# A second folding of the softmax exponentials on GpSimd in a decoder layer

## The chip, the cores and the metric

The kernel runs on one core of a Trainium2 chip. The metric is the device time of one execution in microseconds (us); the time before is the median of three runs. The trace comes from one further, profiled execution. A change in this kernel's time of less than about 0.5% can't be told from none.

## The reference

The reference is one decoder layer over 16 batches of 256 rows of 128 values: a linear-attention block, a cross-attention block, and a feed-forward block on values rounded to a 4-bit grid, each followed by a residual and a layer norm. The change touches only the softmax of the cross-attention, which has 16 heads and a context of R = 64 rows:

```
q = (x @ Wq).reshape(B, L, H, DH).transpose(0, 2, 1, 3)
k = (context @ Wk).reshape(B, R, H, DH).transpose(0, 2, 1, 3)
...
scores = jnp.einsum('bhld,bhrd->bhlr', q, k) * SCALE
attn = jax.nn.softmax(scores, axis=-1)
out = jnp.einsum('bhlr,bhrd->bhld', attn, v)
```

Everything is float32. A softmax row needs the sum of 64 exponentials for each of the 16 heads.

## The kernel before

Each engine runs an instruction stream of its own, written out by hand, and the streams meet at semaphores. Rows lie on the 128 partitions, so a batch of 256 rows is two tiles, t = 0 and t = 1. The work is a software pipeline over the batches: in iteration i, TensorE, VectorE (DVE), ScalarE (ACT) and GpSimd (POOL) work at once on batch i (linear attention), i-1 (its norm, the scores and exponentials of tile 0), i-2 (the rest of the softmax and the cross-attention output), i-3 to i-5 (quantisation, feed-forward, store). Iterations 0 to 5 are unrolled and carry the weight preparation between the batches' work, 6 to 15 are a hardware loop, 16 is unrolled again, and a drain written out by hand ends the kernel. No scheduler decides anything: an instruction whose semaphores are not there holds up all that stands behind it on its engine.

The softmax of tile t of batch b goes through these steps. The scores (128 x 1024) stand in PSUM. DVE takes the maxima (`smax`, L1099), TensorE subtracts them, ACT writes the exponentials `pe` (L775). POOL's `fold_halves` (L474 to L483) adds the second 32 of each head's 64 exponentials to the first 32, from `pe` to `phalf`; `phalf` lies in the space of the weight `xo_w`, and so the trace names it xo_w. DVE's `score_sums` (L1102, trace line L1104) sums the 32 numbers per head into `ssum`, `score_reciprocals` (L1111) makes `srec`, and POOL's `probabilities` (L491) multiplies `pe` by it into `pn` (in the trace fw_c for t = 0 and fw_v for t = 1).

What stands around these steps:

- POOL, t = 0: the norm factors of the linear attention (`veps_attn` L515, `nmean_attn` L527, `rstd_attn` L521, `shift_attn` L535), then the fold, `ya_g` (L541), `x_dequantise` (L499), `za` (L548), the probabilities of t = 0 (L491), and after them `veps_post_attn` (L515).
- DVE, t = 0: the last quantisation steps of x (`xt` L952; L954, whose output the trace names wT), then `ssum`, the feed-forward residual (L1160, named xk_w), `srec`, `stats_ffn`, `fk` (L1024), `stats_post_attn` (L1066, which waits for `za`), and `smax` of t = 1.
- POOL, t = 1: four small operations, the fold, `rstd_ffn` (L521), `kn` (L470, which waits for the last `krn`), the probabilities of t = 1.
- DVE, t = 1: the reciprocal square root of the key norms, nine small steps `kyy` (L1050), `kxyy` (L1052), `krn` (L1055) each of which waits for the one before, then `ssum`, `hg` (L1138), `srec`, `h`.

Of the kernel before, what the change touches and what calls it, by code (L numbers as in the profile page):

```python
# [24 lines left out]
ALU = mybir.AluOpType  # L25
ACT = mybir.ActivationFunctionType
AX = mybir.AxisListType

P = 128
# [3 lines left out]
def decoder_layer(nc, x, ctx_in, aWq, abq, aWk, abk, aWv, abv, aWo, abo, gamma, beta,  # L33
                  xWq, xWk, xWv, xWo, w_gate, w_up, w_down, out):
    B, L, D = x.shape
    R = ctx_in.shape[1]
    T = L // P
    HA = 16
    DA = D // HA
    HX = 16  # L40
# [23 lines left out]
    with es:  # L64
        def sb(name, shape, dt=FP32):
            return es.enter_context(nc.sbuf_tensor(name, shape, dt))
# [4 lines left out]
        def sem(name):  # L71
            return es.enter_context(nc.semaphore(name))
# [81 lines left out]
        ssum = sb("ssum", [P, T, HX])  # L154
# [3 lines left out]
        phalf = tuple(xo_w[:, :, :].rearrange("p j n -> p (j n)")[:, t * HX * R // 2:(t + 1) * HX * R // 2]  # L158
                      for t in range(T))
        pT = (ctx_rows[:, :, :], wT[:, 1, :, :])  # L160
        yx = sb("yx", [P, T, P])
        x2 = sb("x2", [P, T, P])

# [9 lines left out]
        h = sb("h", [P, T, I])  # L173
# [74 lines left out]
        sd_made = sem("sd_made")  # L248
        pe_made = sem("pe_made")
        fold_made = sem("fold_made")  # L250
        ssum_made = sem("ssum_made")
        srec_made = sem("srec_made")
        pn_made = sem("pn_made")
# [36 lines left out]
        def late(b):  # L290

            return not isinstance(b, int) or b > 0
# [15 lines left out]
                 for n, (kind, i) in enumerate(units)]  # L308
        split_units = [n for n, u in enumerate(units) if u[0] in SPLIT]
        unit_at = {(k, i): n for n, (k, i, _) in enumerate(units)}  # L310

        NS = EARLY + HX
# [98 lines left out]
        def _(pool):  # L411
            ge = nc.gpsimd
# [61 lines left out]
            def fold_halves(b, t):  # L474

                pool.wait_ge(pe_made, T * b + t + 1)
                if not late(b):
                    pool.wait_ge(unit_made, unit_at[("H", (1, 1))] + 1)
                if late(b):
                    pool.wait_ge(ssum_made, T * (b - 1) + t + 1)  # L480
                p4 = pe_[:, t, :].rearrange("p (h s r) -> p h s r", h=HX, s=2)
                ge.tensor_tensor(phalf[t].rearrange("p (h r) -> p h r", h=HX), p4[:, :, 0, :], p4[:, :, 1, :],  # L482
                                 ALU.add).then_inc(fold_made, 1)  # L483

            def probabilities(b, t):
                pool.wait_ge(srec_made, T * b + t + 1)
                if not late(b):
                    pool.wait_ge(fw_step, 7)
                if late(b):
                    pool.wait_ge(pT_made, T * (b - 1) + t + 1)  # L490
                ge.tensor_tensor(pn[t].rearrange("p (h r) -> p h r", h=HX),  # L491
                                 pe_[:, t, :].rearrange("p (h r) -> p h r", h=HX),
                                 srec[:, t, :].unsqueeze(2).to_broadcast([P, HX, R]), ALU.mult).then_inc(pn_made, 1)
# [56 lines left out]
            def iteration(i):  # L550
# [15 lines left out]
                if b2 is not None:  # L566
                    fold_halves(b2, 1)
# [27 lines left out]
                if b1 is not None:  # L595
                    fold_halves(b1, 0)
# [11 lines left out]
            probabilities(B - 1, 0)  # L608
            variance_eps("cross", B - 2, eps_ln)
            fold_halves(B - 1, 1)  # L610
            minus_mean("cross", B - 2)
            rstd_of("cross", B - 2)
# [311 lines left out]
        def _(dve):  # L924
            ve = nc.vector
# [174 lines left out]
                                 negate=True).then_inc(smax_made, 1)  # L1100

            def score_sums(b, t):  # L1102
                dve.wait_ge(fold_made, T * b + t + 1)
                ve.tensor_reduce(ssum[:, t, :], phalf[t].rearrange("p (h r) -> p h r", h=HX), AX.X,  # L1104
                                 ALU.add).then_inc(ssum_made, 1)

            def score_reciprocals(b, t):
# [61 lines left out]
            def iteration(i):  # L1169
# [10 lines left out]
                if b3 is not None:  # L1180
                    score_sums(b3, 1)
# [68 lines left out]
                if b2 is not None:  # L1250
                    score_sums(b2, 0)
# [45 lines left out]
            iteration(B)  # L1297

            score_sums(B - 2, 1)
            score_reciprocals(B - 2, 1)  # L1300
            gate_times(B - 4, 1)
# [466 lines left out]
```

## Time and profile before

| | us |
|---|---|
| median of 3 runs | 439.4 |
| lowest, highest | 437.44, 439.61 |
| profiled execution | 440.09 |
| its span in the trace | 438.4 |
| GpSimd busy | 296.2 (68%) |
| VectorE busy | 358.3 (82%) |
| ScalarE busy | 254.7 (58%) |
| TensorE matmuls busy | 375.9 (86%) |

Busy time is an average over a start of about 42 us (loads and weight preparation), some 75 us in which weight preparation and batches mix, a steady part from 119 to 357 us, and a drain. In the steady part each iteration repeats the one before to within a few hundredths of a microsecond, so one iteration read closely stands for all of them. An instruction's duration in the trace runs from its start on the engine to its end; it includes time in which it stands still inside the engine, so the same instruction can show two durations. Consecutive instructions of one engine without a wait between them overlap by about 0.05 us on GpSimd and 0.1 us on VectorE, so a place in a stream is read from start to start.

### The profile page before, as it was taken

To read this page: it belongs to the slowest core of one execution; us is meant where nothing else is said; L and a number is where in the kernel's file an instruction comes from. 1 tells how busy PE (TensorE), PEld (TensorE's weight loads), DVE (VectorE), ACT (ScalarE), POOL (GpSimd) and SP (SyncE) were. 2 spreads that over 40 slices of the span, in tenths; PEclk is the share of its full clock that TensorE was granted. 3 is DMA by queue.
4 is the path that set the end of the run, shared out by engine and by line. 5 is a ranking of instruction groups with operands and counts; after the bars stand their busy time and mean duration, and the time that the engine had idled before them with its cause. 6 is when DMAs were issued, how large, how long until landed. Compare 5 with 4: busy or idle time off the path is not lost. (4 is left out here: it accounts for less than half of the span.)

```text
span 438.4 us, 8439 instructions
## 1 busy us (share of the span) xinstructions
PE 375.9 (86%) x2089; PEld 269.2 (61%) x2089; DVE 358.3 (82%) x941; ACT 254.7 (58%) x499; POOL 296.2 (68%) x468
## 2 busy tenths in 40 slices
PE   2499797899999999999999999999999989878463
PEld 2487565675757575757575858585848575546243
DVE  1738777669999999999999999999999997865661
ACT  1543646567576767676766666666666655545222
POOL 2003557667888888888888888888888889453031
PEclk9889999999999999999999999999999999988655
DMA  8400000000000000000000000000000000000000
GB/s 245 113 1 13 1 13 0 13 14 0 12 4 24 1 24 0 24 0 24 0 24 0 24 0 24 0 24 0 24 0 24 0 14 1 14 0 12 1 12 25
DMA packets 13684, 8.22 MB, mean 19 GB/s; under 512 B 992, under 2 KB 13280, under 8 KB 13664
## 3 DMA queue, kind: packets, MB, share of 16 engines
q1 hardware_dynamic: 13376, 6.93, 5.6%
q10 hardware_dynamic: 288, 1.05, 0.8%
q8 instruction: 9, 0.15, 0.2%
q14 instruction: 11, 0.09, 0.1%
HBM read 5.88 MB, written 2.10 MB: 18 GB/s over the span
## 5 line engine op out<-in xcount | busy, mean ns | idle before, releaser
L1553 PE MATMUL S<-M,x1T 128*128 (+1 forms) x128 | 60.3, 593 | 0.0
L1593 PE MATMUL F<-w_gu,wT 128*128 128x352 f32 x128 | 48.5, 503 | 7.3 <-DVE h L1144 3.5
L482 POOL TENSOR_TENSOR xo_w<-pe 128x512 f32<-128x512 f32 x32 | 42.9, 1340 | 4.1 <-ACT pe L775 3.1
L470 POOL TENSOR_TENSOR kn<-fk,krn 128x256 f32<-128x256 f32 x16 | 11.1, 692 | 48.0 <-DVE krn L1055 48.0
L1593 PEld LDWEIGHTS F<-w_gu,wT 128*128 128x128 f32 x128 | 22.7, 197 | 33.1 <-DVE h L1144 16.5
L1099 DVE TENSOR_REDUCE smax<-S 128x16 fp32r<-128x1024 f32 x32 | 39.1, 1221 | 4.6 <-PE S L1553 2.4
L507 POOL TENSOR_TENSOR wT<-wT,hs 128x704 f32<-128x704 f32 x16 | 22.2, 1387 | 27.7 <-DVE wT L954 27.7
L491 POOL TENSOR_TENSOR fw_v<-pe,srec 128x1024 f32<-128x1024 f32 x16 | 30.4, 1902 | 9.4 <-DVE srec L1111 9.4
L775 ACT ACTIVATE pe<-S 128x1024 f32<-128x1024 f32 x32 | 32.5, 1015 | 5.0 <-PE S L1561 4.9
L1576 PE MATMUL A<-vo,ctx_rows 128*128 128x128 f32 x256 | 33.0, 285 | 1.2 <-issue 1.2
L1576 PEld LDWEIGHTS A<-vo,ctx_rows 128*128 128x128 f32 x256 | 31.5, 201 | 1.4 <-issue 1.4
L1553 PEld LDWEIGHTS S<-M,x1T 128*128 128x128 f32 x128 | 22.1, 191 | 15.5 <-issue 15.3
L1576 PEld LDWEIGHTS A<-vo,wT 128*128 128x128 f32 x256 | 30.9, 192 | 1.1 <-ACT wT L781 0.3
L1576 PE MATMUL A<-vo,wT 128*128 128x128 f32 x256 | 31.4, 276 | 0.0
L1543 PE MATMUL TP<-HW,ctx_cur 128*64 128x512 f32 x128 | 31.0, 605 | 0.0
L491 POOL TENSOR_TENSOR fw_c<-pe,srec 128x1024 f32<-128x1024 f32 x16 | 30.4, 1898 | 0.7 <-DVE srec L1111 0.7
L1608 PE MATMUL F<-w_dn,hT 128*128 128x128 f32 x192 | 27.0, 295 | 3.2 <-ACT hT L814 3.1
L1608 PEld LDWEIGHTS F<-w_dn,hT 128*128 128x128 f32 x192 | 26.0, 209 | 5.5 <-ACT hT L814 4.9
L808 ACT ACTIVATE fw<-F 128x352 f32<-128x352 f32 x32 | 14.9, 464 | 20.2 <-PE F L1593 20.2
L1561 PE MATMUL S<-smax,ident_r 128*128 128x512 f32 x64 | 24.2, 459 | 2.2 <-DVE smax L1099 2.1
L1104 DVE TENSOR_REDUCE ssum<-xo_w 128x16 f32<-128x512 f32 x32 | 21.7, 678 | 4.6 <-POOL xo_w L482 4.6
L720 ACT ACTIVATE kvo<-A 128x128 f32<-128x128 f32 x16 | 4.4, 278 | 33.1 <-PE A L1519 33.1
(189 smaller groups left out, 1051.8 us busy)
## 6 DMA issues: line engine op xcount, KB each, us to landing
x_sb<-in_x SPq DMA_DIRECT2D x16, 128.0 KB, 2.1
out<-xv_w SPq DMA_DIRECT2D x16, 128.0 KB, 1.8
xk_w<-in_L_xattn_Wk ACTq DMA_DIRECT2D x1, 512.0 KB, 4.3
ctx_rows<-in_ctx SPq DMA_DIRECT2D x1, 512.0 KB, 7.4
xv_w<-in_L_xattn_Wv ACTq DMA_DIRECT2D x1, 512.0 KB, 6.8
xq_w<-in_L_xattn_Wq SPq DMA_DIRECT2D x1, 512.0 KB, 8.0
xo_w<-in_L_xattn_Wo SPq DMA_DIRECT2D x1, 512.0 KB, 8.5
fw<-in_L_ffn_w_gate SPq DMA_DIRECT2D x3, 64.0 KB, 3.3
```

The source lines that it names most:

```text
L482: ge.tensor_tensor(phalf[t].rearrange("p (h r) -> p h r", h=HX), p4[:, :, 0, :], p4[:, :, 1, :], ALU.add).then_inc(fold_made, 1)
L491: ge.tensor_tensor(pn[t].rearrange("p (h r) -> p h r", h=HX), pe_[:, t, :].rearrange("p (h r) -> p h r", h=HX), srec[:, t, :].unsqueeze(2) ...
L507: ge.tensor_tensor(hfp4[:, :, :].rearrange("p t (n k) -> p (t n) k", k=BLK), hg4.rearrange("p (n k) -> p n k", k=BLK), hs[:, :].unsqueeze( ...
L775: sc.activation(pe_[:, t, :], S[:, :], ACT.Exp, scale=SCALE).then_inc(pe_made, 1)
L1099: ve.tensor_reduce(smax[:, t, :], S[:, :].rearrange("p (h r) -> p h r", h=HX), AX.X, ALU.max, negate=True).then_inc(smax_made, 1)
L1104: ve.tensor_reduce(ssum[:, t, :], phalf[t].rearrange("p (h r) -> p h r", h=HX), AX.X, ALU.add).then_inc(ssum_made, 1)
L1543: last = te.matmul(TP[par * R:par * R + R, half * BANK:half * BANK + BANK], ctx_cur[:, :], HW[:, par, 4 * half:4 * half + 4, :], start=Tru ...
L1553: last = te.matmul(S[:, half * BANK:half * BANK + BANK], x1T[:, t * P:t * P + P], M[:, HC * half:HC * half + HC, bass.ds(b * R, R)], start ...
L1561: last = te.matmul(S[:, half * BANK:half * BANK + BANK], ident_r[:, :], smax[:, t, HC * half:HC * half + HC].unsqueeze(2).to_broadcast([P, ...
L1576: last = te.matmul(A2[:, t * P:t * P + P], pT[t][:, j, :], vo[:, j, :], start=(j == 0), stop=(j == NJ - 1))
L1593: last = te.matmul(bk[:, 0:I], xfT[:, t * P:t * P + P], w_gu[:, m, :], start=True, stop=True)
L1608: last = te.matmul(F0[:, t * P:t * P + P], hT[:, t, k, :], w_dn[:, k, :], start=(k == 0), stop=(k == NK - 1))
```

## The change

GpSimd gets a second addition after each fold: `phalf` (32 numbers per head) is folded to `pquarter` (16 per head), a new buffer of 2 x 256 numbers per partition. The second addition waits for the first by its semaphore `fold_made`. VectorE's `score_sums` reads `pquarter` instead of `phalf`, and waits for the new semaphore `quarter_made`. The first fold, which waited for the sum of the batch before (`ssum_made`), now waits for the second fold of the batch before, and the second fold for that sum.

```diff
@@ -158,6 +158,7 @@
         pT = (ctx_rows[:, :, :], wT[:, 1, :, :])
+        pquarter = sb("pquarter", [P, T, HX * R // 4])
@@ -477,10 +479,16 @@
                 if late(b):
-                    pool.wait_ge(ssum_made, T * (b - 1) + t + 1)
+                    pool.wait_ge(quarter_made, T * (b - 1) + t + 1)
                 p4 = pe_[:, t, :].rearrange("p (h s r) -> p h s r", h=HX, s=2)
                 ge.tensor_tensor(phalf[t].rearrange("p (h r) -> p h r", h=HX), p4[:, :, 0, :], p4[:, :, 1, :],
                                  ALU.add).then_inc(fold_made, 1)
+                pool.wait_ge(fold_made, T * b + t + 1)
+                if late(b):
+                    pool.wait_ge(ssum_made, T * (b - 1) + t + 1)
+                p4 = phalf[t].rearrange("p (h s r) -> p h s r", h=HX, s=2)
+                ge.tensor_tensor(pquarter[:, t, :].rearrange("p (h r) -> p h r", h=HX), p4[:, :, 0, :], p4[:, :, 1, :],
+                                 ALU.add).then_inc(quarter_made, 1)
@@ -1100,8 +1108,8 @@
             def score_sums(b, t):
-                dve.wait_ge(fold_made, T * b + t + 1)
-                ve.tensor_reduce(ssum[:, t, :], phalf[t].rearrange("p (h r) -> p h r", h=HX), AX.X,
+                dve.wait_ge(quarter_made, T * b + t + 1)
+                ve.tensor_reduce(ssum[:, t, :], pquarter[:, t, :].rearrange("p (h r) -> p h r", h=HX), AX.X,
                                  ALU.add).then_inc(ssum_made, 1)
```

No other engine's stream changes. GpSimd's stream around tile 0 in the loop, before:

```order
L521 TENSOR_TENSOR rstd_attn<-veps_attn,neg_half 128x2 [waits ya_normed,rstd_step_attn]
L535 TENSOR_TENSOR shift_attn<-nmean_attn,rstd_attn 128x2 [waits ya_normed,rstd_step_attn,shift_step_attn]
L482 TENSOR_TENSOR xo_w<-pe 128x512 [waits ssum_made,pe_made]
L541 TENSOR_TENSOR ya_g<-ya_n,gamma_row 128x256 [waits za_step,ya_normed]
L496 ISA
L499 TENSOR_TENSOR fw<-wT,xs 128x256 [waits xfT_made,x2q_step]
```

The same place in the changed kernel (its lines from 482 on are numbered two to eight higher):

```order
L529 TENSOR_TENSOR rstd_attn<-veps_attn,neg_half 128x2 [waits ya_normed,rstd_step_attn]
L543 TENSOR_TENSOR shift_attn<-nmean_attn,rstd_attn 128x2 [waits ya_normed,rstd_step_attn,shift_step_attn]
L484 TENSOR_TENSOR xo_w<-pe 128x512 [waits quarter_made,pe_made]
L490 TENSOR_TENSOR pquarter<-xo_w 128x256 [waits ssum_made,fold_made]
L549 TENSOR_TENSOR ya_g<-ya_n,gamma_row 128x256 [waits za_step,ya_normed]
L504 ISA
L507 TENSOR_TENSOR fw<-wT,xs 128x256 [waits xfT_made,x2q_step]
```

One instruction more stands between the fold and `ya_g`. GpSimd's stream around tile 1, before:

```order
L515 TENSOR_TENSOR veps_cross<-mv_cross,eps_ln 128x2 [waits rstd_step_cross,mv_made_cross]
L476 REGISTER_ALU
L482 TENSOR_TENSOR xo_w<-pe 128x512 [waits ssum_made,pe_made]
L518 REGISTER_ALU
L521 TENSOR_TENSOR rstd_ffn<-veps_ffn,neg_half 128x2 [waits out_made,rstd_step_ffn]
L467 ISA
L470 TENSOR_TENSOR kn<-fk,krn 128x256 [waits kvT_made,krn_step]
```

And in the changed kernel:

```order
L523 TENSOR_TENSOR veps_cross<-mv_cross,eps_ln 128x2 [waits rstd_step_cross,mv_made_cross]
L478 REGISTER_ALU
L484 TENSOR_TENSOR xo_w<-pe 128x512 [waits quarter_made,pe_made]
L490 TENSOR_TENSOR pquarter<-xo_w 128x256 [waits ssum_made,fold_made]
L526 REGISTER_ALU
L529 TENSOR_TENSOR rstd_ffn<-veps_ffn,neg_half 128x2 [waits out_made,rstd_step_ffn]
L469 ISA
L472 TENSOR_TENSOR kn<-fk,krn 128x256 [waits kvT_made,krn_step]
```

The new instruction stands between the fold and `rstd_ffn`. VectorE's stream has the same rows as before; only `ssum` reads and waits for something else.

## Rows read from the trace of the kernel before

**Rows 1.** Page, engines: busy us (share of the span) and instructions.

```profile
PE 375.9 (86%) x2089; PEld 269.2 (61%) x2089; DVE 358.3 (82%) x941; ACT 254.7 (58%) x499; POOL 296.2 (68%) x468
```

**Rows 2.** Busy time in the steady part: stretch, its length, busy us (instructions), clock, DMA.

```profile
119.00:357.25 238.25, 224.55 (x1297) 160.04 (x1298) 227.82 (x618) 160.04 (x318) 201.91 (x308) 1.00 0.04 11
```

**Rows 3.** Timeline of GpSimd: start, us, instruction, [idle before and its releaser].

```profile
119.09 0.19 POOL L515 TENSOR_TENSOR veps_attn<-mv_attn,eps_attn 128x2 f32<-128x2 f32 x1 [0.26 <-DVE mv_attn L1070]
...
357.34 0.20 POOL L515 TENSOR_TENSOR veps_attn<-mv_attn,eps_attn 128x2 f32<-128x2 f32 x1 [0.26 <-DVE mv_attn L1070]
```

**Rows 4.** Groups by line and shape: count, busy us, mean ns, idle before.

```profile
L1104 DVE TENSOR_REDUCE ssum<-xo_w 128x16 f32<-128x512 f32 x32 | 21.7, 678 | 4.6 <-POOL xo_w L482 4.6
L941 DVE TENSOR_REDUCE xam<-x 128x16 f32<-128x256 f32 x16 | 6.6, 411 | 4.8 <-ACT x L738 4.8
```

**Rows 5.** One line's instructions: count, shortest/median/longest ns, first and last start.

```profile
L954 DVE SCALAR_TENSOR_TENSOR wT<-xc,xt x16: 417/1336/1343, 100.9 to 409.0; 128x256 f32<-128x256 f32 x16
```

**Rows 6.** Timeline of VectorE at tile 0 in a steady iteration.

```profile
229.28 1.34 DVE L954 SCALAR_TENSOR_TENSOR wT<-xc,xt 128x256 f32<-128x256 f32 x1
230.54 0.68 DVE L1104 TENSOR_REDUCE ssum<-xo_w 128x16 f32<-128x512 f32 x1
...
231.98 0.40 DVE L1024 SCALAR_TENSOR_TENSOR fk<-ek,A 128x256 f32<-128x256 f32 x1
232.50 0.49 DVE L1066 BATCH_NORM_STATS2 stats_post_attn<-za 128x6 f32<-128x128 f32 x2
```

**Rows 7.** Timeline of GpSimd at tile 0 in the same iteration.

```profile
228.88 1.45 POOL L482 TENSOR_TENSOR xo_w<-pe 128x512 f32<-128x512 f32 x1
230.30 0.91 POOL L541 TENSOR_TENSOR ya_g<-ya_n,gamma_row 128x256 f32<-128x256 f32 x1
231.17 0.61 POOL L499 TENSOR_TENSOR fw<-wT,xs 128x256 f32<-128x256 f32 x1
231.75 0.72 POOL L548 TENSOR_TENSOR za<-ya_g,x_beta 128x256 f32<-128x256 f32 x1
...
234.64 0.20 POOL L515 TENSOR_TENSOR veps_post_attn<-mv_post_attn,eps_ln 128x2 f32<-128x2 f32 x1 [0.31 <-DVE mv_post_attn L1070]
```

**Rows 8.** Timeline of VectorE at tile 1 in a steady iteration.

```profile
215.25 1.05 DVE L1055 SCALAR_TENSOR_TENSOR krn<-kxyy,krn 128x32 f32<-128x32 f32 x1
216.33 0.19 DVE L1050 TENSOR_TENSOR kyy<-krn 128x32 f32<-128x32 f32 x1
216.55 0.19 DVE L1052 SCALAR_TENSOR_TENSOR kxyy<-kyy,kse 128x32 f32<-128x32 f32 x1
...
217.58 0.69 DVE L1104 TENSOR_REDUCE ssum<-xo_w 128x16 f32<-128x512 f32 x1
```

**Rows 9.** Timeline of GpSimd at tile 1 in the same iteration.

```profile
214.97 1.27 POOL L482 TENSOR_TENSOR xo_w<-pe 128x512 f32<-128x512 f32 x1
216.20 0.70 POOL L521 TENSOR_TENSOR rstd_ffn<-veps_ffn,neg_half 128x2 f32<-128x2 f32 x1
217.73 0.63 POOL L470 TENSOR_TENSOR kn<-fk,krn 128x256 f32<-128x256 f32 x1 [0.83 <-DVE krn L1055]
218.93 1.90 POOL L491 TENSOR_TENSOR fw_v<-pe,srec 128x1024 f32<-128x1024 f32 x1 [0.58 <-DVE srec L1111]
```

**Rows 10.** Timeline of VectorE: first and last long small step of tile 1.

```profile
69.06 1.29 DVE L1052 SCALAR_TENSOR_TENSOR kxyy<-kyy,kse 128x32 f32<-128x32 f32 x1
...
345.13 1.14 DVE L1055 SCALAR_TENSOR_TENSOR krn<-kxyy,krn 128x32 f32<-128x32 f32 x1
```

**Rows 11.** Timeline of VectorE, outside the steady part: sums that waited for a fold.

```profile
63.88 0.69 DVE L1104 TENSOR_REDUCE ssum<-xo_w 128x16 f32<-128x512 f32 x1 [1.83 <-POOL xo_w L482]
...
367.77 0.69 DVE L1104 TENSOR_REDUCE ssum<-xo_w 128x16 f32<-128x512 f32 x1 [1.52 <-POOL xo_w L482]
...
387.34 0.69 DVE L1104 TENSOR_REDUCE ssum<-xo_w 128x16 f32<-128x512 f32 x1 [1.26 <-POOL xo_w L482]
388.69 0.52 DVE L1138 SCALAR_TENSOR_TENSOR hg<-fw,F 128x352 f32<-128x352 f32 x1 [0.66 <-ACT fw L808]
```

More of the change, by code:

```diff
@@ L250, in decoder_layer @@
         fold_made = sem("fold_made")
+        quarter_made = sem("quarter_made")
         ssum_made = sem("ssum_made")
```

## The prediction

> **What bounds the kernel now.** I read the busy shares first, then the busy time of the steady part, then the timelines of VectorE and GpSimd through one iteration. The shares alone [rows 1] suggest the change: GpSimd is busy 68% of the span and VectorE 82%. The steady part sharpens that. From the first to the last veps_attn it holds 11 iterations, (357.34 - 119.09) / 11 = 21.66 us each [rows 3]. In it VectorE is busy 227.8 of 238.25 us, 20.7 us per iteration, TensorE 224.6 and GpSimd 201.9, 18.4 us per iteration [rows 2]. VectorE sets the pace: in its timeline of an iteration I found one idle stretch of 0.19 us, and the rest runs start to start. GpSimd has about 3.3 us free per iteration. Were that all, moving work from VectorE to GpSimd would pay.
>
> The timelines show two things that the shares hide. First, VectorE is not slow by its own work alone. L954 on 256 elements takes 0.42 us when alone and 1.34 us in the median [rows 5]. In the steady iteration it starts at 229.28 and ends at 230.62, just behind the fold that runs from 228.88 to 230.33 [rows 6, 7]: it stands still until GpSimd's fold is done, then needs 0.29 us. The krn step at tile 1 does the same: 0.19 us of work takes 1.05 us, from 215.25 to 216.30, and the fold ends at 216.24 [rows 8, 9]. The other way round too: ya_g behind the fold starts at 230.30, while L954 runs, and takes 0.91 us against 0.72 for the like-sized za [rows 7]. So an operation of VectorE that reads two SBUF operands and a reading GpSimd operation exclude each other, and the fold is in effect on VectorE's path already.
>
> The Trainium skill states this as a rule (SBUF — State Buffer, section "Who interferes with whom"): the second read port is an exclusive lock held for the whole instruction, taken by a GpSimd instruction that reads SBUF or by a VectorE one with two SBUF inputs, while a tensor_reduce never takes part. By that rule the longer GpSimd time at the folds costs VectorE time, while the shortened sum frees no port. The trace agrees (1.34 against 0.42 us); without the rule the case would be the third rival below.
>
> Second, both folds stand where VectorE is about to need them. ssum at tile 0 starts at 230.54, 0.2 us behind the fold, and stats_post_attn at 232.50 starts as za ends, 231.75 + 0.72 = 232.47 [rows 6, 7].
>
> **Removed.** 32 sums over 512 elements at 0.678 us become sums over 256. The nearest row is xam, a reduction of 256 elements to 16, with 0.411 us [rows 4]. I take that, so 0.27 us less each; the bounds are 0 (should the time not follow the elements) and 0.34 (half of the old time).
>
> **Added.** 32 GpSimd additions with an output of 256. The trace has three kinds of that size: 0.61 us (L499, one operand broadcast), 0.72 us (za, two full operands), 0.91 us (ya_g, with its standing still) [rows 7]. The fold of 512 takes 1.27 us [rows 9]. The new one has two full operands, so it is nearest to za: 0.72 us; the ends are 0.61 and 0.91. It must wait for the fold's own completion. From the ends and starts of such dependent GpSimd pairs I estimate 0.08 us, and GpSimd's next instruction loses its usual overlap of 0.04 us, not more. The new slot is therefore about 0.80 us from start to start. The changed waits of the first fold cost nothing: they are for the batch before, an iteration earlier.
>
> **Tile 0, steady.** The fold ends at 230.33. L954, which stood waiting, gets the port and ends at 230.62 as before. The second fold is ready at about 230.41 and gets the port behind L954, as ya_g does now. ya_g now ends at 231.17 + 0.04 = 231.21 [rows 7]. The second fold takes exactly that place and ends there (0.72 us, the za duration, from 230.49), and ya_g, fw and za follow, each later by 0.72 - 0.04 = 0.68 us. On VectorE ssum can't start before 231.25 instead of 230.54: 0.71 us lost, 0.27 won back by its shorter duration, so VectorE runs 0.44 us late. Behind ssum stand the residual, srec, stats_ffn and fk. They end at 231.98 + 0.40 + 0.44 = 232.82. But stats_post_attn waits for za, which now ends at 232.47 + 0.68 = 233.15. So VectorE is late by 0.68 us from here on, and the win at ssum is swallowed by that wait. GpSimd's next wait is for VectorE (veps_post_attn, 0.31 us idle before it [rows 7]), so the loss isn't caught up. The 11 steady iterations hold 12 such folds, one behind each veps_attn from 119.09 to 357.34 us [rows 3]: 12 x 0.68 = 8.2 us.
>
> **Tile 1.** The fold starts at 214.97 and ends at 216.24 [rows 9]. Behind it on GpSimd stands rstd_ffn, which has two elements and hardly touches the port: kxyy at 216.55 runs in 0.19 us beside it [rows 8, 9]. Now the second fold stands there, ready at 216.32, and VectorE wants kyy at 216.33. If the fold is first, kyy ends at 216.32 + 0.72 + 0.05 = 217.09 instead of 216.52, 0.57 us late (the 0.05 is how far behind the fold the blocked krn ended, 216.30 against 216.24). If kyy is first, kxyy is blocked and loses about 0.42 us. I take 0.57. The six steps, ssum and what follows are a chain without gaps, so this goes through; ssum finds its input long done and gives 0.27 back. Net +0.30 us. GpSimd's own delay is covered here: kn waits 0.83 us for krn before [rows 9], enough for the 0.80 us slot. The steps stand beside the fold in 14 of 16 cases, from the kxyy at 69.06 to the krn at 345.13, each with one long step [rows 10]; in the last two batches no key norms are left. So 14 x 0.30 = 4.2 us.
>
> **Outside the steady part.** Three sums waited for their fold with nothing else to do [rows 11]. There the second fold is on the path with its whole 0.80 us less 0.27: 0.53 us each. Of these the one at 387.34 is covered, since hg behind it waits for ScalarE until 388.69 [rows 11]. The tile 0 fold of the iteration before the steady part, between the two, is a weaker form of the steady case, for which I estimate 0.5 us. Together 2 x 0.53 + 0.5 = 1.6 us. In the drain the other sums have room, for nothing.
>
> **Sum.** 8.2 + 4.2 + 1.6 = +14.0 us. Against the profiled execution (span 438.4 and 1.7 us around it, 440.09) that is 454.1 us. The median of the runs is 0.7 us lower, 439.4, so as a median 453.4, which I round to 453.5, +3.2%. An iteration goes from 21.66 to about 22.64 us.
>
> The low end: the addition at 0.61 us, so 0.57 at each tile 0; at tile 1 kxyy is blocked and not kyy, for 0.42 - 0.11 = 0.31 us, and the sum saves 0.34. 12 x 0.57 - 14 x 0.03 + 1.1 outside = 7.5 us, 446.9 as a median. The high end: 0.91 us, and a saving of 0. 12 x 0.87 + 14 x 0.76 + 2.7 outside = 23.7 us, 463.1.
>
> **Rivals.**
> First, faster: VectorE's shorter sums decide. Place: the two ssum slots of each iteration. Price: 28 sums x 0.27 = -7.6 us, 431.8 us. For it: VectorE is the busiest engine in the steady part and GpSimd has 3.3 us free. It needs GpSimd at tile 0 to come early enough that the second fold ends before L954 does, which the trace denies: L954 ends behind the first fold already, since that fold follows a chain from VectorE's own mv_attn (veps, rstd, shift). It would decide if that chain ran 0.8 us ahead. 5%.
>
> Second, GpSimd becomes the bound and both slots land in full: 2 x 0.80 = 1.6 us in each of 14 iterations, +22.4, 461.8 us. For it: GpSimd and VectorE take turns waiting for each other and the free time is scattered. Against: at tile 1 the 0.83 us before kn is room. 10%.
>
> Third, no blocking at tile 1: the six short steps slip beside the new fold as they do beside rstd_ffn. Then tile 1 wins 14 x 0.27 = 3.8 instead of losing 4.2: 8.2 - 3.8 + 1.6 = +6.0, 445.4 us. For it: most short steps show 0.19 us. Against: one step in each iteration shows 1.05. 12%.
>
> Fourth, savings and waits cancel, or the streams settle with another phase in which L954 no longer meets the fold: 439 to 441 us. 5%.
>
> **Chances.** My forecast 68%. What a measurement can tell from no change is about 0.5%, 2.2 us. Faster 0.05, within 0.5% 0.04, slower 0.91. The range for 8 in 10 takes in the third rival and the greater part of the way to the upper end, which needs both costs at their worst: 445 to 460 us. The other 1% is for what none of these names.
>
> **What would show it.** Right, if the steady iteration is 22.6 us; a pquarter addition of about 0.72 us; the ssum of tile 0 with an idle stretch of 0.6 to 0.7 us released by pquarter; stats_post_attn waiting for za; a second long step (0.7 us) behind the long krn; ssum at 0.41. Wrong, if kyy and kxyy stay at 0.19 (third rival), if kn waits for GpSimd's own work and not for krn (second), or if ssum at tile 0 starts without idle time (first).

## The result, and the profile after

The change makes the kernel slower: 451.41 us median (451.31 to 452.64, 4 runs) against 438.62 (437.44 to 439.61, 4 runs), a ratio of 1.0293 with a 95% interval of 1.0258 to 1.0328. Forecast were 453.5 us and 3.2%. The profiled execution after took 452.64 us, 450.8 of them span, 12.4 more than the span before.

GpSimd's timeline gives the steady iteration, as [rows 3] did before (start, us, instruction, idle before and releaser):

```profile
120.75 0.19 POOL L523 TENSOR_TENSOR veps_attn<-mv_attn,eps_attn 128x2 f32<-128x2 f32 x1 [0.26 <-DVE mv_attn L1078]
...
366.82 0.19 POOL L523 TENSOR_TENSOR veps_attn<-mv_attn,eps_attn 128x2 f32<-128x2 f32 x1 [0.26 <-DVE mv_attn L1078]
```

(366.82 - 120.75) / 11 = 22.37 us, 0.71 more than before. So the span's 12.4 us are 7.8 in the 11 steady iterations, 1.7 ahead of them (120.75 against 119.09), and 2.9 behind. Busy time of the steady part after, columns as in [rows 2]:

```profile
120.75:366.82 246.07, 226.15 (x1297) 158.17 (x1297) 226.22 (x617) 160.54 (x318) 216.72 (x330) 1.00 0.04 11
```

VectorE's busy time barely falls, from 227.8 to 226.2 us in 11 iterations, though 22 sums are 0.26 us shorter each (5.7 us). Two small steps of tile 1, shown below, eat most of what is missing: kxyy stands still 0.41 us longer and krn 0.14 less in each iteration, 3.0 us in 11. GpSimd's busy time grows by 14.8 us. And VectorE, which had no idle stretch at tile 0 up to stats_post_attn, now waits there twice. VectorE at tile 0, answering to [rows 6]:

```profile
212.19 1.33 DVE L962 SCALAR_TENSOR_TENSOR wT<-xc,xt 128x256 f32<-128x256 f32 x1
214.15 0.42 DVE L1112 TENSOR_REDUCE ssum<-pquarter 128x16 f32<-128x256 f32 x1 [0.62 <-POOL pquarter L490]
...
215.34 0.40 DVE L1032 SCALAR_TENSOR_TENSOR fk<-ek,A 128x256 f32<-128x256 f32 x1
216.10 0.49 DVE L1074 BATCH_NORM_STATS2 stats_post_attn<-za 128x6 f32<-128x128 f32 x2 [0.35 <-POOL za L556]
```

GpSimd at tile 0, answering to [rows 7]:

```profile
211.79 1.45 POOL L484 TENSOR_TENSOR xo_w<-pe 128x512 f32<-128x512 f32 x1
213.32 0.80 POOL L490 TENSOR_TENSOR pquarter<-xo_w 128x256 f32<-128x256 f32 x1
214.08 0.72 POOL L549 TENSOR_TENSOR ya_g<-ya_n,gamma_row 128x256 f32<-128x256 f32 x1
...
215.34 0.72 POOL L556 TENSOR_TENSOR za<-ya_g,x_beta 128x256 f32<-128x256 f32 x1
...
218.24 0.19 POOL L523 TENSOR_TENSOR veps_post_attn<-mv_post_attn,eps_ln 128x2 f32<-128x2 f32 x1 [0.32 <-DVE mv_post_attn L1078]
```

The sum is shorter (0.42 for 0.68 us) but waits 0.62 us. What counts is the second wait: from the fold's start to za's start were 231.75 - 228.88 = 2.87 us, now 215.34 - 211.79 = 3.55, which is 0.68 later, and stats_post_attn starts as za ends. The second fold takes the place in which ya_g stood still behind L954 (ya_g 0.91 before, 0.72 now). From the fold's start to the end of that place are 214.12 - 211.79 = 2.33 us, as the prediction had it (231.21 - 228.88).

VectorE at tile 1, answering to [rows 8]:

```profile
220.50 0.91 DVE L1063 SCALAR_TENSOR_TENSOR krn<-kxyy,krn 128x32 f32<-128x32 f32 x1
221.44 0.19 DVE L1058 TENSOR_TENSOR kyy<-krn 128x32 f32<-128x32 f32 x1
221.67 0.60 DVE L1060 SCALAR_TENSOR_TENSOR kxyy<-kyy,kse 128x32 f32<-128x32 f32 x1
...
223.11 0.42 DVE L1112 TENSOR_REDUCE ssum<-pquarter 128x16 f32<-128x256 f32 x1
```

GpSimd at tile 1, answering to [rows 9]:

```profile
219.94 0.20 POOL L523 TENSOR_TENSOR veps_cross<-mv_cross,eps_ln 128x2 f32<-128x2 f32 x1
220.09 1.27 POOL L484 TENSOR_TENSOR xo_w<-pe 128x512 f32<-128x512 f32 x1
221.44 0.79 POOL L490 TENSOR_TENSOR pquarter<-xo_w 128x256 f32<-128x256 f32 x1
222.19 0.69 POOL L529 TENSOR_TENSOR rstd_ffn<-veps_ffn,neg_half 128x2 f32<-128x2 f32 x1
223.25 0.63 POOL L472 TENSOR_TENSOR kn<-fk,krn 128x256 f32<-128x256 f32 x1 [0.38 <-DVE krn L1063]
```

A second small step stands still: kyy and the second fold start together, kyy gets through, and kxyy takes 0.60 us instead of 0.19, ending 0.04 us behind the second fold. But krn ahead of it stands still for less, 0.91 instead of 1.05 us. So it is in the last 10 of the 14 batches in which the steps meet the folds. In three before them, the last of which is in the first steady iteration, it is kyy that stands still (0.61, 0.78 and 0.78 us); one of them:

```profile
109.41 0.78 DVE L1058 TENSOR_TENSOR kyy<-krn 128x32 f32<-128x32 f32 x1
```

### The profile page after: what moved, and what is told of

Same layout as the page of the kernel before. It is cut to its first block and busy times, and to the rows that moved or that the text cites. A ratio compares the mean times of both kernels' runs of the same rounds, so it can differ in the third digit from the quotient of the medians.

```text
span 450.8 us, 8501 instructions
## 1 busy us (share of the span) xinstructions
PE 377.2 (84%) x2089; PEld 265.9 (59%) x2089; DVE 355.4 (79%) x941; ACT 255.0 (57%) x499; POOL 318.3 (71%) x500
## 3 DMA queue, kind: packets, MB, share of 16 engines
q10 hardware_dynamic: 288, 1.05, 0.7%
## 5 line engine op out<-in xcount | busy, mean ns | idle before, releaser
L1601 PE MATMUL F<-w_gu,wT 128*128 128x352 f32 x128 | 49.8, 514 | 7.3 <-DVE h L1152 3.5
L1584 PEld LDWEIGHTS A<-vo,wT 128*128 128x128 f32 x256 | 31.9, 197 | 1.0 <-ACT wT L789 0.2
L1584 PE MATMUL A<-vo,ctx_rows 128*128 128x128 f32 x256 | 31.3, 276 | 1.2 <-issue 1.2
L1584 PEld LDWEIGHTS A<-vo,ctx_rows 128*128 128x128 f32 x256 | 29.9, 192 | 1.4 <-issue 1.4
L816 ACT ACTIVATE fw<-F 128x352 f32<-128x352 f32 x32 | 14.8, 463 | 21.6 <-PE F L1601 21.6
L490 POOL TENSOR_TENSOR pquarter<-xo_w 128x256 f32<-128x256 f32 x32 | 24.9, 780 | 2.5
L1569 PE MATMUL S<-smax,ident_r 128*128 128x512 f32 x64 | 22.2, 429 | 4.7 <-DVE smax L1107 2.4
```

The source lines that it names most:

```text
L490: ge.tensor_tensor(pquarter[:, t, :].rearrange("p (h r) -> p h r", h=HX), p4[:, :, 0, :], p4[:, :, 1, :], ALU.add).then_inc(quarter_made, 1)
L1569: last = te.matmul(S[:, half * BANK:half * BANK + BANK], ident_r[:, :], smax[:, t, HC * half:HC * half + HC].unsqueeze(2).to_broadcast([P, ...
L1584: last = te.matmul(A2[:, t * P:t * P + P], pT[t][:, j, :], vo[:, j, :], start=(j == 0), stop=(j == NJ - 1))
L1601: last = te.matmul(bk[:, 0:I], xfT[:, t * P:t * P + P], w_gu[:, m, :], start=True, stop=True)
```

## The experiments

Each steady iteration below is the distance of two consecutive veps_attn starts around 210 us in that run's timeline; by the same measure the kernel before has 227.37 - 205.71 = 21.66 us and the changed one 232.64 - 210.28 = 22.36. Start and drain add one to three microseconds that differ between profiled executions, so where theories lie close the iteration decides. The medians of e1, e3 and e4 lie 2.1 to 2.3 us above the totals that were expected, though their iterations are within 0.1 us; e7's lies 3.3 above, and there the iteration is off as well.

| run | median us | ratio to before (95%) | steady iteration |
|---|---|---|---|
| changed kernel | 451.41 | 1.029 (1.026 to 1.033) | 22.36 |
| e1, tile 0 only | 448.78 | 1.023 (1.018 to 1.028) | 232.22 - 210.01 = 22.21 |
| e2, tile 1 only | 441.34 | 1.004 (1.001 to 1.008) | 229.48 - 207.70 = 21.78 |
| e3, second fold unused | 455.65 | 1.036 (1.029 to 1.043) | 234.72 - 212.09 = 22.63 |
| e4, a power in its place | 447.09 | 1.017 (1.011 to 1.023) | 230.28 - 208.09 = 22.19 |
| e5, short sums alone | 434.22 | 0.992 (0.990 to 0.994) | 224.99 - 203.59 = 21.40 |
| e6, no fold | 431.53 | 0.983 (0.978 to 0.988) | 222.53 - 201.41 = 21.12 |
| e7, no fold at tile 0 | 437.76 | 0.999 (0.997 to 1.001) | 226.40 - 204.77 = 21.63 |
| e8, no fold at tile 1 | 433.69 | 0.990 (0.987 to 0.992) | 224.77 - 203.44 = 21.33 |

The kernel before had 438.2 us (13 runs) beside e1 to e4 and 437.88 (14 runs) beside e5 to e8.

**One tile at a time.** e1 and e2 make the second fold for one tile; the edit for e1:

```diff
+                if t == 0:
+                    pool.wait_ge(fold_made, T * b + t + 1)
...
+                    ge.tensor_tensor(pquarter[:, t, :].rearrange("p (h r) -> p h r", h=HX), p4[:, :, 0, :],
+                                     p4[:, :, 1, :], ALU.add).then_inc(quarter_made, 1)
```

> The second fold and the shorter sum for tile 0 alone; tile 1 as in the kernel before. Theory A (the second fold pushes za, the operation that VectorE's stats_post_attn waits for, back by 0.68 us, and the fold of tile 1, which waited 0.13 us for ScalarE's exponentials, gives 0.14 us of it back): a steady iteration of 22.20 us, total about 446.5 us. Rival B (the two tiles' costs are independent, 0.68 for tile 0): 22.34 us and 448. Rival C (tile 0 costs only what its sum waits, 0.62 less the 0.27 it is shorter): 22.0 us and 443.5.

> The second fold and the shorter sum for tile 1 alone; tile 0 as in the kernel before. Theory A (the second fold blocks one small step of the reciprocal square root by 0.41 us, the sum is 0.27 us shorter, and here the fold of tile 1 still waits for the exponentials): 21.80 us per steady iteration, total 440.5 us; with kyy blocked instead, 21.96 us and 442. Rival C (no blocking, only the shorter sum counts): 21.39 us and 434.5 us.

The iterations are 22.21 and 21.78 us, theory A's 22.20 and 21.80. Tile 0 alone costs 0.55 us, tile 1 alone 0.12, together 0.67 of the 0.70 that the whole change costs. e1's total is 2 us above what was expected; in its profiled execution the start is 2.1 us longer than before (veps_attn at 121.20 against 119.09) and what lies behind the last veps_attn 2.0 us (83.07 against 81.06), which the steady part doesn't explain. In e2 krn takes 1.05 us as before, and kxyy 0.61:

```profile
217.22 1.05 DVE L1067 SCALAR_TENSOR_TENSOR krn<-kxyy,krn 128x32 f32<-128x32 f32 x1
218.30 0.19 DVE L1062 TENSOR_TENSOR kyy<-krn 128x32 f32<-128x32 f32 x1
218.53 0.61 DVE L1064 SCALAR_TENSOR_TENSOR kxyy<-kyy,kse 128x32 f32<-128x32 f32 x1
```

So at tile 1 the blocking costs 0.42 us and the sum gives 0.27 back, which would leave 0.15 where 0.12 are measured, and the shorter stand of krn appears only where tile 0 is late: in e1 it is 0.92 us.

**Wait, place in the queue or port.** e3 keeps both second folds but sums from the first ones; the edit without the wait of the second fold for the sum (`ssum_made`), which moves to the first fold:

```diff
-                dve.wait_ge(quarter_made, T * b + t + 1)
-                ve.tensor_reduce(ssum[:, t, :], pquarter[:, t, :].rearrange("p (h r) -> p h r", h=HX), AX.X,
+                dve.wait_ge(fold_made, T * b + t + 1)
+                ve.tensor_reduce(ssum[:, t, :], phalf[t].rearrange("p (h r) -> p h r", h=HX), AX.X,
```

> Both second folds are made, but VectorE sums 32 numbers per head from the first fold and waits for that alone, as before. Theory A (za late by 0.68 us whoever reads the fold; at tile 1 0.14 back, 0.41 blocked, and no 0.27 won): a steady iteration of 22.62 us, total about 453.5 us, slower than the changed kernel. Rival C (what costs is that the sum waits for the second fold): tile 0 costs nothing, about 22.0 us and 443 us, faster than the changed kernel.

22.63 us, where 22.62 was expected. VectorE at tile 0, in its timeline:

```profile
215.26 0.67 DVE L1111 TENSOR_REDUCE ssum<-xo_w 128x16 f32<-128x512 f32 x1
...
216.70 0.40 DVE L1031 SCALAR_TENSOR_TENSOR fk<-ek,A 128x256 f32<-128x256 f32 x1
217.91 0.48 DVE L1073 BATCH_NORM_STATS2 stats_post_attn<-za 128x6 f32<-128x128 f32 x2 [0.81 <-POOL za L555]
```

The sum no longer waits, and the loss isn't smaller: it turns up whole at stats_post_attn, which starts 0.81 us behind fk's end; before it was 0.12 [rows 6], so 0.69 more. So the wait of 0.62 us at the sum is not what costs at tile 0; za's lateness is. e4 is the kernel before with an operation of nearly the same length in the second fold's place which hardly reads:

```diff
+                ge.tensor_tensor(pquarter[:, t, 0:2], eps_ln[:, 0:2], neg_half[:, 0:2], ALU.pow).then_inc(quarter_made, 1)
```

> As the run before it, but each second fold is replaced by a GpSimd operation on 2 elements (a power, 0.69 to 0.72 us as rstd has) that takes as long and hardly reads SBUF; the sums are as in the kernel before. Theory A (at tile 0 the place in GpSimd's queue costs, 0.58 us since L954 doesn't hold it up; at tile 1 the blocking costs, and here nothing is blocked, so 0.14 comes back): 22.10 us per steady iteration, total about 445 us, kxyy and kyy at 0.19 us. Rival D (a place in the queue is all, no exclusion at a port): as with the unused fold, 22.6 us and 453 us.

22.19 us, 0.44 less than e3. GpSimd at tile 0 and tile 1, and VectorE at tile 1:

```profile
209.60 1.46 POOL L485 TENSOR_TENSOR xo_w<-pe 128x512 f32<-128x512 f32 x1
211.14 0.76 POOL L488 TENSOR_TENSOR pquarter<-eps_ln,neg_half 128x2 f32<-128x2 f32 x1
...
213.14 0.72 POOL L553 TENSOR_TENSOR za<-ya_g,x_beta 128x256 f32<-128x256 f32 x1
...
219.23 0.76 POOL L488 TENSOR_TENSOR pquarter<-eps_ln,neg_half 128x2 f32<-128x2 f32 x1
```

```profile
219.24 0.19 DVE L1055 TENSOR_TENSOR kyy<-krn 128x32 f32<-128x32 f32 x1
219.46 0.19 DVE L1057 SCALAR_TENSOR_TENSOR kxyy<-kyy,kse 128x32 f32<-128x32 f32 x1
```

GpSimd is busy as long and at the same place, and kxyy is back at 0.19 us. That shows the exclusion at tile 1: a busy GpSimd isn't enough for it, the addition over 256 elements blocks and the power over 2 doesn't. Whether the number of elements or the kind of operation makes the difference, no run separates. At tile 0 the place in the queue costs nearly as before: fold to za is 213.14 - 209.60 = 3.54 us, so 0.67, not the 0.58 expected, since the power takes 0.76 us.

**What the shorter sum is worth.** e5 is the kernel before with half of each sum left out:

```diff
-                ve.tensor_reduce(ssum[:, t, :], phalf[t].rearrange("p (h r) -> p h r", h=HX), AX.X,
+                ve.tensor_reduce(ssum[:, t, :], phalf[t].rearrange("p (h r) -> p h r", h=HX)[:, :, 0:R // 4], AX.X,
```

> The kernel before, with VectorE summing only the first 16 of the 32 numbers per head: half of the exponentials are left out of the sum, no second fold is made. It is the gain of the shorter sums alone. Theory A (at tile 0 stats_post_attn waits for za anyway, so only tile 1's 0.27 us counts): 21.36 us per steady iteration, total about 434.5 us. Rival (VectorE is the bound and both count, 0.54 us): 21.12 us and 431.5 us.

21.40 us: 0.26 of a possible 0.54. Even free of charge the change could bring 3.7 us (434.22 against 437.88), as tile 0's win ends in the wait for za. (e5's sums are half of what they should be; it is a run for its time alone.)

**The other direction.** e6 to e8 drop the fold for both tiles or one, and VectorE sums 64 numbers per head. The edit of e6; in e7 and e8 the tuple `(0, 1)` is `(0,)` or `(1,)`:

```diff
             def fold_halves(b, t):
+                if t in (0, 1):
+                    return
...
             def score_sums(b, t):
-                dve.wait_ge(fold_made, T * b + t + 1)
-                ve.tensor_reduce(ssum[:, t, :], phalf[t].rearrange("p (h r) -> p h r", h=HX), AX.X,
+                if t in (0, 1):
+                    dve.wait_ge(pe_made, T * b + t + 1)
+                    src = pe_[:, t, :]
...
+                ve.tensor_reduce(ssum[:, t, :], src.rearrange("p (h r) -> p h r", h=HX), AX.X,
```

> The other direction: no fold at all, VectorE sums all 64 exponentials per head from pe. Its sums take 1.22 us instead of 0.68 (as smax over 1024 elements does), but L954 and krn no longer stand still behind a fold (0.92 and 0.86 us). Theory A: 0.38 won at tile 0 and 0.32 at tile 1, 20.96 us per steady iteration, or 21.2 where TensorE, busy 20.4 us of it, becomes the bound; total 430 to 433 us. Rival (VectorE's work decides, port or not): 2 x 0.54 more, 22.7 us and 452 us.

> No fold for tile 0 alone. Theory A: 21.3 us per steady iteration, total 434.5 us, L954 at 0.42 us. Rival (VectorE's work decides): 22.2 us and 445 us.

> No fold for tile 1 alone. Theory A: 21.34 us per steady iteration, total 435 us, every krn step at 0.19 us. Rival (VectorE's work decides): 22.2 us and 445 us.

e6 beats both kernels, 431.53 us, 1.7% under the one before, though it gives VectorE 32 x 0.54 = 17 us more to sum. From its VectorE timeline:

```profile
212.08 0.19 DVE L1057 SCALAR_TENSOR_TENSOR krn<-kxyy,krn 128x32 f32<-128x32 f32 x1
212.21 1.22 DVE L1111 TENSOR_REDUCE ssum<-pe 128x16 f32<-128x1024 f32 x1
...
224.44 0.39 DVE L956 SCALAR_TENSOR_TENSOR wT<-xc,xt 128x256 f32<-128x256 f32 x1
```

L954 (here L956) takes 0.39 instead of 1.34 us and all krn steps 0.19: the two stands of 0.95 and 0.86 us outweigh the two longer sums. e8 is as expected, 21.33 for 21.34 us, and shows this for tile 1 by itself: nothing there waited for the fold before (ssum started 1.3 us behind it [rows 8, 9]), and the 0.33 us won are the 0.86 of the stand less the 0.54 of the longer sum. At tile 0 dropping the fold does two things at once, it frees L954 and it lets za come earlier on GpSimd; by the timelines both are needed, as stats_post_attn started 0.03 us behind za's end [rows 6, 7], but no run separates them. e7 missed: 21.63 us, no gain, 21.3 expected. First the row of the kernel before for `smax`, then e7's VectorE timeline:

```profile
211.53 1.23 DVE L1099 TENSOR_REDUCE smax<-S 128x16 fp32r<-128x1024 f32 x1 [0.19 <-DVE stats_post_attn L1066]
```


```profile
206.68 0.39 DVE L956 SCALAR_TENSOR_TENSOR wT<-xc,xt 128x256 f32<-128x256 f32 x1
206.99 1.21 DVE L1111 TENSOR_REDUCE ssum<-pe 128x16 f32<-128x1024 f32 x1
208.49 0.42 DVE L1167 TENSOR_TENSOR xk_w<-F,xq_w 128x256 f32<-128x256 f32 x1 [0.29 <-PE F L1615]
...
210.35 1.23 DVE L1101 TENSOR_REDUCE smax<-S 128x16 fp32r<-128x1024 f32 x1 [0.20 <-PE S L1560]
...
214.08 1.26 DVE L1057 SCALAR_TENSOR_TENSOR krn<-kxyy,krn 128x32 f32<-128x32 f32 x1
```

VectorE saves 0.95 us at L954 and gives 0.54 back at the sum. Then it waits 0.29 us for TensorE's F, a wait that it didn't have before; the 0.20 us ahead of smax are not new (0.19 before). It reaches smax 210.35 - 204.77 = 5.58 us behind veps_attn, before 211.53 - 205.71 = 5.82, so 0.24 us early. Of these krn, which comes earlier to a fold that doesn't, gives back 0.21 us (1.26 for 1.05). In e6, with no fold in krn's way, tile 0's win stays (21.12 against e8's 21.33).

## Why the prediction was right, and where a term was off

The sign, the mechanism and the size held: +12.8 us between the medians, +14.0 forecast. That the total is so near is in part luck: over the profiled spans the 11 steady iterations cost 7.8 us and not 10.8, and what lies outside them 4.6 and not 3.2. Point by point:

- **VectorE sets the pace, and the fold is in its way**: held. L954 takes 1.33 us after as it took 1.34 before, e5 shows that time taken off VectorE at tile 1 is won whole, and e8 what a fold costs there.
- **Prices**: the sum 0.418 us (0.41 taken), the second fold 0.73 us at its shortest and 0.79 in the median (0.72 taken; the rest is standing behind L954 or kyy).
- **Tile 0, 0.68 us each**: held to the hundredth, as did the claim that the sum's own saving would be swallowed at stats_post_attn; e3 shows that the sum's wait could be left out without a gain.
- **Tile 1, 0.30 us each**: mis-sized, and the term of the sum that was off. In the steady iterations it should have been 0.02 or 0.03 in company with tile 0 (22.36 or, over all 11, 22.37 us, less 21.66 and 0.68). The prediction let kyy be blocked for 0.57. That came in the three batches from 90 to 132 us (0.42 to 0.59 us of stand), but in the 10 from 154 us on kyy got through and kxyy lost 0.41, the prediction's lower case. And it took the fold's place behind veps_cross as fixed. Before, the fold waited for ScalarE's exponentials; the timelines of ScalarE, before and after:

```profile
213.87 1.02 ACT L775 ACTIVATE pe<-S 128x1024 f32<-128x1024 f32 x1
```

```profile
218.88 1.02 ACT L783 ACTIVATE pe<-S 128x1024 f32<-128x1024 f32 x1 [0.41 <-PE S L1569]
```

  Before they end at 214.89, and the fold starts 0.08 us later [rows 9]. After they end at 219.90 and the fold, at 220.09, comes right behind veps_cross. Tile 0's lateness used up that wait: before, ScalarE came to this exponential without an idle stretch, now it idles 0.41 us ahead of it. So krn stands still 0.14 us less. So 0.41 - 0.27 - 0.14 = 0.00, where e2, with the wait still there, has 0.12.
- **Outside the steady part, 1.6 us**, plus the tile 0 fold and the three tile 1 folds of the sum that fall outside: forecast 3.2 in all (1.9 ahead, 1.2 behind), measured 1.7 ahead and 2.9 behind. Of the latter 1.26 us lie in one stretch of the drain with the same work in it. Its busy times, before and after:

```profile
401.38:409.55 8.17, 3.77 (x15) 1.83 (x13) 4.58 (x19) 2.81 (x7) 1.86 (x6) 0.92 0.00 0
```

```profile
412.57:422.00 9.43, 5.04 (x15) 2.33 (x13) 4.58 (x19) 2.81 (x7) 1.85 (x6) 0.76 0.00 0
```

  TensorE's granted clock is 0.92 in the one and 0.76 in the other, and the same 15 matmuls take 3.77 and 5.04 us. The means mix the two levels, 2.4 and 1.2 GHz: the last four of these matmuls follow 1.84 us (before) and 1.83 us (after) of idle TensorE and take 1.45 us before, at full clock, and 2.72 us after, at 0.50. The same four take 1.45 us in e2 and e5 too, and 2.71 or 2.72 in the other six experiments, among them e6, which is faster than the kernel before. So the late clock isn't bound to a slower kernel; why it differs there is open, and whether executions without a profile have it isn't known. The prediction had no term for it, and in the profiled span it hides part of the mis-sized term.
- **The rivals**: the third (no blocking at tile 1) falls with kxyy at 0.60 us, the second with 0.38 us of kn's wait still there, the first with the 0.62 us at the sum. e5 shows that the first would have been worth half of its price, 3.7 us and not 7.6, had it been free. The fourth (within 2 us of the time before) falls with the +12.8 us.
- **Small slips of the sum**: the chances of the forecast and of the four rivals add up to 100% already, so nothing was left for the 1% that none of them names; and the terms of the high end add up to 23.8, not 23.7 us.

## What to carry to other kernels

A helper engine that blocks the engine it helps, as GpSimd's additions do here, is not free capacity: before work is moved from VectorE to GpSimd, look for VectorE instructions whose duration varies with the same shape, and see which GpSimd instruction ends as they do. Price the move by what stands behind the new instruction in its queue, not by the busy shares, and by the next join of the two streams, where a win of one engine alone is lost. Where such stands are found, test the opposite move as well; here it was the one that paid (e6, 1.7%), though not for tile 0 alone (e7).

## What the runs showed of the hardware that was not expected

A step on 32 elements took 0.60 to 1.29 us beside a GpSimd addition (1.29 in [rows 10]; 0.19 alone), and 0.19 us beside a GpSimd power of 0.76 us on two elements. The Trainium skill (SBUF — State Buffer, section "SBUF: two separate sides") lets a GpSimd instruction hold the port pair for the whole instruction once it has started. For the additions the traces agree; the power also reads SBUF, and there kyy and kxyy run beside it at 0.19 us (e4), so here the measurement decides against the whole instruction. A lock for only the time in which operands are streamed would fit both; no run shows that directly.

Nor is a second operand from SBUF needed for a VectorE instruction to stand still. The scale step hs of the feed-forward quantisation (L944) reads one operand, ham. It takes 0.19 us at its shortest and 0.60 in the median, and in the kernel before its row beside GpSimd's multiplication [rows 9, L491] ends at 220.87, 0.04 us behind that multiplication's 220.83:

```profile
220.28 0.59 DVE L944 TENSOR_SCALAR hs<-ham 128x44 f32<-128x44 f32 x1
```

The prediction named two operands as the condition; that was too narrow, though no term of its sum hangs on it.
